# One carried buffer of 32 KB, the stores of the choices by expert moved into the experts' first dispatch, and four banks for the turned choices

## What is computed

```python
# layer 1: a long convolution (Hyena style)
u  = x @ W_in + b_in;  x0, x1, v = split(short_conv(u), 3);  v = v * x1
k  = gen_filter(8192, ...)                       # a small sine MLP
v  = causal_fft_conv(v, k, filter_bias)          # over all 8192 positions
x  = layernorm(x + (v * x0) @ W_out + b_out)

# layer 2: experts; 256 groups of t = 32 tokens; 32 experts x 4 sets = 128
logits = einsum('bgtd,des->bgtes', grouped, controller) + tie
perm   = (logits == max over the group's 32 tokens)   # 0 or 1
dispatched   = einsum('bgtd,bgtes->bgesd', grouped, perm)
inner        = relu(einsum('bgesd,desf->bgesf', dispatched, f1) + bias)
intermediate = einsum('bgesf,esfd->bgesd', inner, f2)
out = einsum('bgesd,bgtes->bgtd', intermediate, perm)
x   = layernorm(x + out)
```

## Time and profile before

| what | value |
|---|---|
| median of three executions | 2247.01 us |
| the profiled execution, its own time | 2249.36 us |
| its span, first to last instruction | 2247.6 us |
| mean granted TensorE clock | 0.909 |
| busy: PE, VectorE, ScalarE, GpSimd | 85%, 63%, 42%, 23% |
| DMA moved | 513.73 MB, 229 GB/s over the span |

### The profile page before, as it was taken

How to read it: one execution, slowest core, us unless ns; L and a number is a source line. 1 busy time by engine, 2 the same in 40 slices (tenths; PEclk the granted TensorE clock), 3 DMA queues, 4 the chain that set the end, 5 groups by cost and what they waited for, 6 DMA issues and landing times. The chain is left out here.

```text
span 2247.6 us, 34871 instructions
## 1 busy us (share of the span) xinstructions
PE 1907.3 (85%) x12342; PEld 1292.9 (58%) x12342; DVE 1406.1 (63%) x2748; ACT 933.2 (42%) x1755; POOL 512.2 (23%) x410
## 2 busy tenths in 40 slices
PE   7999999999998798999979999995767676576444
PEld 6777777777776443444458888884636352352000
DVE  5877777787788454545558889884434353364343
ACT  4444544444444344454445555552323242242222
POOL 0100110001000044454445555550302020020000
PEclk9999999999999899999989999997878897697555
DMA  5233333423342577888767777765697999999999
GB/s 166 74 111 134 104 113 108 143 102 113 113 135 85 181 206 224 219 246 230 193 206 249 241 248 234 239 212 200 247 385 282 389 355 407 405 332 410 371 391 338
DMA packets 287297, 513.73 MB, mean 229 GB/s; under 512 B 26479, under 2 KB 105365, under 8 KB 278805
## 3 DMA queue, kind: packets, MB, share of 16 engines
q1 hardware_dynamic: 277909, 494.71, 65.3%
q10 hardware_dynamic: 9216, 16.78, 2.0%
HBM read 309.78 MB, written 201.62 MB: 228 GB/s over the span
## 5 line engine op out<-in xcount | busy, mean ns | idle before, releaser
L90 PE MATMUL p_pu<-p_xT_high,p_win_high 128*128 128x512 f32 (+1 forms) x816 | 329.6, 404 | 14.4 <-DVE p_win_low L85 12.1
L91 PE MATMUL p_pu<-p_xT_high,p_win_low 128*128 128x512 f32 (+1 forms) x816 | 313.2, 384 | 0.0
L92 PE MATMUL p_pu<-p_xT_low,p_win_high 128*128 128x512 f32 (+1 forms) x816 | 312.8, 383 | 0.0
L447 ACT ACTIVATE p_t<-p_pu,p_tbias,p_taps 128x512 f32<-128x512 f32 (+1 forms) x192 | 146.5, 763 | 358.3 <-PE p_pu L92 357.4
L564 DVE SCALAR_TENSOR_TENSOR p_t<-p_pu,p_taps,p_t 128x256 f32<-128x256 f32 (+1 forms) x384 | 208.5, 543 | 6.9
L85 POOL TENSOR_TENSOR p_xT_low<-p_xT,p_xT_high 128x2048 fp32r<-128x2048 f32 (+1 forms) x16 | 71.1, 4441 | 618.1 <-ACT p_xT_high L80 618.1
L849 POOL TENSOR_TENSOR q_y<-q_y 128x512 f32<-128x512 f32 x128 | 160.2, 1272 | 195.1 <-DVE q_y L870 195.1
L90 PEld LDWEIGHTS p_pu<-p_xT_high,p_win_high 128*128 128x128 f32 x816 | 155.0, 190 | 47.0 <-DVE p_xT_low L85 10.3
L92 PEld LDWEIGHTS p_pu<-p_xT_low,p_win_high 128*128 128x128 f32 x816 | 154.7, 190 | 32.8
L91 PEld LDWEIGHTS p_pu<-p_xT_high,p_win_low 128*128 128x128 f32 x816 | 155.1, 190 | 25.4
L1458 PE MATMUL e_pd<-e_taken,e_ff 128*32 128x128 f32 x2048 | 87.6, 326 | 94.4 <-DMA e_ff<-in_L_ffn_f 90.8
(11 more groups left out here) (135 smaller groups left out, 3800.3 us busy)
## 6 DMA issues: line engine op xcount, KB each, us to landing
s_I<-e_out SPq DMA_DIRECT2D x64, 1024.0 KB, 8.4
s_SV<-p_sout SPq DMA_DIRECT2D x128, 256.0 KB, 2.0
q_av<-s_SV SPq DMA_DIRECT2D x64, 512.0 KB, 4.4
s_Z<-q_z SPq DMA_DIRECT2D x128, 256.0 KB, 3.2
o_zin<-s_Z SPq DMA_DIRECT2D x64, 512.0 KB, 4.0
e_ff<-in_L_ffn_f SPq DMA_DIRECT2D x64, 512.0 KB, 9.2
e_inter<-s_I SPq DMA_DIRECT2D x32, 1024.0 KB, 12.7
e_taken<-s_I SPq DMA_DIRECT2D x32, 1024.0 KB, 11.8
```

The source lines that it names most:

```text
L90: pe.matmul(out, a[0], b[0], start=start, stop=False)
L91: pe.matmul(out, a[1], b[0], start=False, stop=False)
L92: return pe.matmul(out, a[0], b[1], start=False, stop=stop)
L447: nc.scalar.activation(t[r][m % 2][:, c], pu[(W + n) % 3][:, c], ACT.Identity, bias=tbias[:, w:w + 1], scale=taps[:, w, 2:3]).then_inc(t_o ...
```

## The change

One buffer K of 128 partitions by 8192 float32 (32 KB a partition) is allocated around all phases. In the front phase it holds `shared` and two of the four `sout`; in the output phase it is `logit`; in the experts' phase it holds `inter` and `res` (columns 0 to 6143) and the weight buffers 2 and 3 (columns 6144 to 8191). The stores to TAKE leave the output phase and are issued from K in the first dispatch of the experts. `took` has four buffers, and the turned choices go to four banks, the two of `pc` being added.

```diff
@@ output_phase @@
-    NZ, NR, NK = 3, 6, 2
+    NZ, NR, NK = 3, 6, 4
...
-        logit = sb("logit", [P, N1, 2, GT])
+        logit = K[:].rearrange("p (n r t) -> p n r t", n=N1, r=2)
...
-        pt = [ps(f"pt{s}", [P, 4, ES]) for s in range(2)]
+        pt = [ps(f"pt{s}", [P, 4, ES]) for s in range(2)] + pc
...
             def store_unit(u):
-                sp.wait_ge(take_ok, ONE + UNITS + u + 1)
-                sp.dma_start(S["TAKE"][:, u * 2 * UG * GT:(u + 1) * 2 * UG * GT],
-                             logit[:, u * UG:(u + 1) * UG].rearrange("p g r t -> p (g r t)")).then_inc(take_st, 16)
                 for b in range(2):
                     sp.wait_ge(took_ok[b], ONE + u + 1)
...
-            sp.wait_ge(take_st, ONE + 16 * UNITS)
...
             def turn_take(v):
                 pe.wait_ge(take_ok, ONE + UNITS + v // 2 + 1)
-                if v >= 2:
-                    pe.wait_ge(took_ok[v % 2], ONE + v // 2)
+                if v == 2:
+                    pe.wait_ge(c_used, ONE + TILES)
+                if v >= 4:
+                    pe.wait_ge(took_ok[v % 2], ONE + v // 2 - 1)
...
@@ experts_phase @@
+    WEIGHTS_OVER = (6, 7)
+    TILES_OVER = (0, 1, 2, 3, 4, 5)
...
-        inter = [sb(f"inter{s}", [P, 4, D]) for s in range(NI)]
+        inter = [K[:, s * 4 * D:(s + 1) * 4 * D].rearrange("p (g d) -> p g d", g=4) for s in range(NI)]
...
-        ff = [sb(f"ff{s}", [P, 2, D]) for s in range(NF)]
+        ff = [sb(f"ff{s}", [P, 2, D])[:] for s in range(2)] + [
+            K[:, s * 2 * D:(s + 1) * 2 * D].rearrange("p (a d) -> p a d", a=2) for s in WEIGHTS_OVER]
...
-        res = [sb(f"res{s}", [P, D]) for s in range(NR)]
+        res = [K[:, (NI * 4 + s) * D:(NI * 4 + s + 1) * D] for s in range(NR)]
...
-            sp.dma_start(side[:], A["side"]).then_inc(consts, 16)
-            sp.dma_start(bias[:], A["ffn_bias"]).then_inc(consts, 16)
...
+            def store_take(u, signal):
+                b = slice(u * 2 * D, (u + 1) * 2 * D)
+                sp.dma_start(S["TAKE"][:, b], K[:, b]).then_inc(signal, 16)
...
             for j in range(NK):
                 load_picks(j)
                 if j < 2:
                     load_pair(0, j)
+                if j == 0:
+                    sp.dma_start(side[:], A["side"]).then_inc(consts, 16)
+                    sp.dma_start(bias[:], A["ffn_bias"]).then_inc(consts, 16)
...
                 if c == 2:
+                    sp.wait_ge(take_out_2, ONE + 16 * len(TILES_OVER))
...
-                    if j == PH // 2 and c == 0:
-                        for n in range(NF):
+                    if c == 0 and PH // 2 <= j < PH // 2 + 2:
+                        load_weights(j - PH // 2)
+                        store_take(WEIGHTS_OVER[j - PH // 2], take_out)
+                    elif c == 0 and PH // 2 < j < PH:
+                        store_take(TILES_OVER[j - PH // 2 - 2], take_out_2)
+                    if j == PH - 1 and c == 0:
+                        sp.wait_ge(take_out, ONE + 16 * len(WEIGHTS_OVER))
+                        for n in range(2, NF):
                             load_weights(n)
...
@@ program @@
+    with nc.sbuf_tensor("k_shared", [P, L], F32) as K:
```

More of the change, by code:

```diff
@@ L134, in output_tables, with front_phase @@
             "x0": [sb(f"x0{s}", [P, DT, P]) for s in range(AHEAD)], "x": [sb(f"x{s}", [P, D]) for s in range(AHEAD)]}
-def front_phase(nc, sem, A, S, F):
+def front_phase(nc, sem, A, S, K, F):
     J = CH // N1
@@ L156, in front_phase @@
         xT_s = [[sb(f"xT_{n}{s}", [P, DT, CH], F32R) for n in ("high", "low")] for s in range(2)]
-        shared = sb("shared", [P, W * HC + 2 * J * D])
+        shared, top = K, W * HC + 2 * J * D
         keep = sb("keep", [P, W, 2, N1 + 1])
@@ L165, in front_phase @@
         dft = [sb(f"dft{s}", [P, J, 2, P]) for s in range(2)]
-        sout = [sb(f"sout{s}", [P, D]) for s in range(NS)]
+        sout = [K[:, top + s * D:top + (s + 1) * D] for s in range(2)] + [sb(f"sout{s}", [P, D])[:] for s in range(2, NS)]
         pos = [sb(f"pos{s}", [6, HC]) for s in range(2)]
@@ L281, in store_s @@
                 sp.wait_ge(sout_ok, ONE + n + 1)
-                sp.dma_start(S["SV"][:, r * N2 + i * J + j, :], sout[n % NS][:]).then_inc(s_st[n % NS], 16)
+                sp.dma_start(S["SV"][:, r * N2 + i * J + j, :], sout[n % NS]).then_inc(s_st[n % NS], 16)
             def store_h(i):
@@ L462, in keep_s @@
                     act.wait_ge(s_st[n % NS], ONE + n // NS * 16)
-                nc.scalar.copy(sout[n % NS][:], pz[n % 2][:]).then_inc(sout_ok, 1)
+                nc.scalar.copy(sout[n % NS], pz[n % 2][:]).then_inc(sout_ok, 1)
             def sine(i, n):
@@ L876, in _, with output_phase @@
                 multiply(p)
-def output_phase(nc, sem, A, S, O):
+def output_phase(nc, sem, A, S, K, O):
     TILES = N2
@@ L913, in output_phase @@
         pl = ps("pl", [P, 2, P])
-        pt = [ps(f"pt{s}", [P, 4, ES]) for s in range(2)]
+        pt = [ps(f"pt{s}", [P, 4, ES]) for s in range(2)] + pc
         z_in, x0_in = ([sem(f"o_{n}{s}") for s in range(NZ)] for n in ("z_in", "x0_in"))
         x_in, x1_st = ([sem(f"o_{n}{s}") for s in range(NR)] for n in ("x_in", "x1_st"))
-        take_st, took_st = sem("o_take_st"), [sem(f"o_took_st{s}") for s in range(NK)]
+        took_st = [sem(f"o_took_st{s}") for s in range(NK)]
         (c_ps, c_used, gate_ok, offs_ok, y1_ok, y_ok, x_sum, o_ps, res_ok, stats_ok, var_ok, std_ok, inv_ok, norm_ok,
@@ L1050, in turn_take @@
                 pe.wait_ge(take_ok, ONE + UNITS + v // 2 + 1)
[L1051 to L1052 removed]
+                if v == 2:
+                    pe.wait_ge(c_used, ONE + TILES)
+                if v >= 4:
+                    pe.wait_ge(took_ok[v % 2], ONE + v // 2 - 1)
                 for b in range(4):
                     g = v * UG // 2 + 2 * b
[L1055 removed]
+                    m = pe.transpose(pt[v % 4][:, b, :], logit[:, g:g + 2].rearrange("p g r t -> p (g r t)"), ident[:])
                 m.then_inc(t_ps, 1)
@@ L1076, in keep_took @@
             copy(took[u % NK][:, :, 4 * b:4 * b + 4].rearrange("p h m e -> p m h e"),
-                 pt[b][:].rearrange("p m (h e) -> p m h e", h=2)).then_inc(took_ok[b], 1)
+                 pt[v % 4][:].rearrange("p m (h e) -> p m h e", h=2)).then_inc(took_ok[b], 1)
         @block.scalar
@@ L1204, in _, with experts_phase @@
             keep_took(dve, dve.tensor_copy, 2 * UNITS - 1)
-def experts_phase(nc, sem, A, S):
+def experts_phase(nc, sem, A, S, K):
     GH = P
@@ L1254, in experts_phase @@
         late = taken[:, 0:NL * LW].rearrange("p (s w) -> p s w", w=LW)
+        take_out, take_out_2 = sem("e_take_out"), sem("e_take_out_2")
         consts, eps_ok = sem("e_consts"), sem("e_eps_ok")
@@ L1283, in inter_of @@
             if m < NT0:
-                return inter[m % NI][:], take[m % NI][:]
+                return inter[m % NI], take[m % NI][:]
             v = late[:, (m - NT0) % NL, :]
@@ L1290, in res_of @@
             if m < NT0:
-                return res[m % NR][:]
+                return res[m % NR]
             return late[:, (m - NT0) % NL, 4 * D + P:5 * D + P]
@@ L1336, in load_weights @@
                     sp.wait_ge(o_ps, ONE + n - NF + 1)
-                sp.dma_start(ff[s][:], A["ffn_f"][:, n % Q]).then_inc(ff_in[s], 16)
+                sp.dma_start(ff[s], A["ffn_f"][:, n % Q]).then_inc(ff_in[s], 16)
             def load_tile(m):
@@ L1344, in load_tile @@
                     sp.wait_ge(c_ps, ONE + m - NI + 1)
-                sp.dma_start(inter[s][:], S["I"][4 * m:4 * m + 4].rearrange("g e d -> e g d")
+                sp.dma_start(inter[s], S["I"][4 * m:4 * m + 4].rearrange("g e d -> e g d")
                              ).then_inc(inter_in[s], 16)
@@ L1349, in load_tile @@
                     sp.wait_ge(res_st[r], ONE + m // NR * 16)
-                sp.dma_start(res[r][:], xr[m]).then_inc(res_in[r], 16)
+                sp.dma_start(res[r], xr[m]).then_inc(res_in[r], 16)
             def load_late(m):
@@ L1621, in run @@
             phase(nc, Semaphores(ctx, nc), A, S, *tables)
[L1623 to L1629, removed]
+    with nc.sbuf_tensor("k_shared", [P, L], F32) as K:
+        with ExitStack() as made:
+            F = front_tables(made, nc)
+            run(front_phase, K, F)
+            O = output_tables(made, nc)
+            run(frequency_phase, F, O)
+            run(output_phase, K, O)
+        run(experts_phase, K)
 def constants():
```

## The result

The changed kernel took 2231.34 us (median of 2231.34, 2229.18 and 2236.01) against 2247.01 before: a ratio of 0.9928, 95% interval 0.9912 to 0.9944, so 15.7 us less by the medians and 12.6 to 19.8 us by the interval. Forecast were 12.2 us less, 2235, with a range of 2229 to 2243. The profiled execution after has a span of 2229.5 us and an own time of 2231.34.

The account below looks back on a forecast made before the run. The prediction took DMA to bound the output tail and the experts' iterations, and the first dispatch to alternate between DMA and products. 9.2 + 0.3 + 2.7 + 0 = 12.2 us off the 2247.01 median gave 2235, range 2229 to 2243.

Parts of the forecast that it names:

- The tail: End of the output phase: without TAKE stores the last TOOK store is issued 9.2 us earlier, granted clock 1.0.
- rival B: Output tail: slow clock holds, turns run at 1.2 GHz, saving 4.6 instead of 9.2 us; 2239.4 us, chance 0.09.
- The start of the experts: First transfers to first product: pair 0 earlier, side and bias behind it; a gain of 0.3 us taken.
- The end of the dispatch: First dispatch: four units instead of six up to picks 7, so they and the first expert product come 2.7 us earlier.
- rival C: Shorter dispatch stall also spares the slow clock after it, and the tail's landing shrinks: 15 us less, 2232, chance 0.10.
- The TAKE stores in the idle stretch: Before the first experts: 10.8 us of stores hidden, weights 2 about 1.0 us late, cost taken as 0.
- Rival D: First dispatch: stores mixed with loads move at 165 GB/s, pushing the experts' first store; 2.9 us slower, 2249.9, chance 0.05.
- Rival A: First dispatch gains nothing: picks 7 no sooner, or late weights 2 and 3 pay it back; 2238 us, chance 0.24.
- The sum: Whole kernel: tail, start, dispatch and TAKE terms together give 12.2 us less, 2235 us; chance 0.52.

Follow-up runs that it names:

- after: The first measurement and profile of the changed kernel, unedited: 2231.34 us against 2247.01 for the kernel before, ratio 0.9928.
- late_takes: Changed kernel with TAKE stores 0 to 5 issued in the second step's dispatch instead of the first: 2232.83 us, ratio 0.9935 to the kernel before.
- best_again: Changed kernel, side and bias first, weights 0 and 1 and TAKE stores 6 and 7 behind picks 7, stores 0 to 5 in second step; second measurement: 2229.9 us.
- weights_split: Kernel before with only its first weights spread (0 at j = 8, 1 at j = 9, 2 and 3 at j = 15): 2241.79 us, ratio 0.9971.
- before_again: Kernel before, measured and profiled once more, unedited: 2250.18 us, ratio 1.0004.
- banks_only: Kernel before with four banks and four took buffers, TAKE still stored in the tail: 2249.25 us, ratio 1.0001.
- after_again: Changed kernel, measured and profiled once more, unedited: 2233.2 us, ratio 0.9929 to the kernel before.
- takes_twice: Changed kernel with TAKE stores 0 to 5 each issued a second time, to an unread scratch tensor: 2241.47 us, ratio 0.9974 to the kernel before.

## Why the prediction was right, and where it was not

The tail: right. Forecast 9.2 us less, found 9.5 in the first pair of profiles and 9.1 in the means. The last store is issued 12.2 us after the first choice instead of 13.2: 0.7 us of that because the second copy came 3.8 us after the first choice and not 4.55 as before, 0.25 because the six copies after it took 7.6 us, not 7.9, although the first of them were held up by slow turns. The queue (1.02 of it in use, 375 GB/s) takes part of it back, and the last store lands 4.7 us later instead of 4.1. The clock was not 1.00 through all the turns, as I had said it would be. In three of the seven profiles that have the whole of the changed tail (after, late_takes, best_again) the second turn took 1.9 and the third 1.7 to 1.8 us, and their tails are 20.3 us; in the other four every turn took 1.0 to 1.1, and the tails are 19.7 to 19.9. So rival B's slow turns happen, but for two turns and some 0.5 us, not for all eight and 4.6 us.

The start of the experts: wrong in sign, and wrong in what it is worth. Forecast was a gain of 0.3; `bias`, issued at 1553.99, landed 3.73 us after that, behind pair 0, and the first product came 1.1 us later than before. My latest landing had been too early by half a microsecond. But this loss costs nothing: the queue sets when pair 6 can begin, and in the means that is 0.6 us sooner than without the edit (21.4 us into the phase instead of 21.9). I had read that the dispatch alternates between DMA and products, and had not asked which of the two sets the time of its first stall.

The end of the dispatch: the mechanism was right, and weights_split shows it. The term of 2.7 us is what the first pair of profiles has, 6.22 to 3.56 us of stall; in the means it is 1.8 (5.5 to 3.65), since the trace that I read had the longest stall of the four. To this comes the clock. In the first pair pairs 6 to 13 took 1.6 us less, and from the resumption to the experts' first product it was 6.60 instead of 7.85 us. That is what rival C said, which I had priced at 1.5 us and seen at one of the two places. But the means have only 0.8 and 0.3 us of it: before_again and banks_only kept the full clock in pairs 6 to 13 without the edit, and after_again took 8.04 us at the end with it. From the phase's first transfer to the first expert product the sum forecast 3.0, and the profiles show 5.6 in the first pair and 3.5 in the means. That 3.5 is so near to 3.0 is in part luck: the stall gave less than its term, and the start and the clock, which I had at 0.3 and at nothing, made up for it.

The TAKE stores in the idle stretch: right. Weights 2 were late by 1.25 us (1.0 forecast), and takes_twice shows how exactly the stretch was filled. The two times behind that wait were both off by nearly the same: weights 2 landed 50.5 us into the phase (53.1 forecast) and were wanted at 49.3 (52.1 forecast), as the queue moved 412 to 414 GB/s where I had charged 390. From 1600 to 1605 it moved 308, under the 350 that I had asked for up to the first store. Rival D is out: the queue moves stores mixed with loads at 412 to 414 GB/s, not at 165. (The rate at which D turns from gain to loss was also reckoned wrongly: a push of 9.5 us lets TAKE take 22.5 us, which is 186 GB/s, not 178.) Rival A is out by the stall. The first step's experts are 0.7 to 1.0 us longer, but the profiles without the edit already scatter from 62.2 to 64.7.

The sum: the means of the touched stages give 9.1 + 3.5 - 1.0 = 11.6 us, and whole profiles differ by 12.5 in the mean, while the times say 15.7 and 15.6, each with an interval that reaches from 12.6 to over 19. The whole profiles fall short of the times because of the executions that were profiled: the two of the changed kernel are 3.2 us above their medians on average, the four others 0.4 below. So 11.6 us are explained by the touched stages and about 4 us are not located. The stretch ahead of the choices scatters by 6 us and that behind the first step by 7, with two profiles of one kernel and four of the other. Over all fourteen profiles the nine with moved stores reach the first choice 1.1 us sooner and take 2.5 us less behind the first step than the five without, which would be most of the missing 4 us; but these stretches differ by 4 to 7 us among profiles of one kind, so this is not shown and stays open. The forecast of 2235 was right in direction and size, and 3.7 us too high.

## What to carry to other kernels

A transfer that bounds one stage can be free in another: look for the stretch in which the queue idles, count it in units of that queue, and keep the data where it is until then. What it may not do is stand ahead of a small load that an engine waits for: the place in the queue was worth 0.9 to 1.6 us for each half megabyte. Before one shortens a start, one should see whether the next stall is set by the engine or by the queue, since in the second case the start is free either way.

## What the runs showed that was not expected

A dispatch whose first product came 1.1 us later into the phase ended earlier. The stall in its middle shrank from 3.66 to 1.49 us, the 64 products after it took 3.84 us, and the eight pairs after it 14.56 instead of 16.2; with side and bias first the stall was 2.72 us and the eight pairs took 16.07. The granted clock goes with it. The four us after the stall in the changed kernel and with side and bias first (columns as in the earlier trace rows):

```profile
1574.00:1578.00 4.00, 3.85 (x68) 3.88 (x70) 1.22 (x1) 1.87 (x2) 2.39 (x5) 1.00 0.81 280
```

```profile
1578.00:1582.00 4.00, 3.96 (x43) 3.99 (x45) 0.36 (x1) 1.01 (x1) 1.33 (x3) 0.60 0.73 262
```

After the shorter stall TensorE kept the full clock and did 68 products in 4 us; after the longer it was granted 0.60 on average, partly the lower level, and did 43. The length of the stall alone does not decide it. Here is the same place in before_again, with a stall as long as in the first profile of this kernel (3.66 us) and the full clock after it:

```profile
1585.72 3.84 PE L1446 MATMUL e_pd<-e_pick,e_out 64*128 64x128 f32 x64 [3.63 <-issue]
```

Over the two stalls of the dispatch in all fourteen profiles, the 64 products after a stall of up to 1.9 us took 3.84 us in all eight cases. After a longer one (2.25 to 6.22 us) they took 5.19 us or more in 17 of 19 cases, and 3.84 in two, before_again (3.63) and banks_only (3.40). So a shorter stall made the full clock likelier, and what else decides it is not shown.
